# Positive part and square of each mixer step on one engine, in place, in a ring of six slots

## The reference

```python
inv_norm = rsqrt(maximum(sum(xf * xf, -1), EPS));  xn = xf * inv_norm
sim = einsum('bic,bjc->bij', xn, xn)
sim = power(relu(sim), 2.0)              # positive part, then square
y = einsum('bij,bjc->bic', sim, t)       # t = x W
x = x + y
```

## Time and profile before

| | us |
|---|---|
| median of 3 runs | 4165.13 |
| lowest and highest run | 4151.47 and 4180.86 |
| span of the profiled execution | 4159.1 |
| PE busy in it | 3515.1 (85%) |
| VectorE busy | 3096.5 (74%) |
| ScalarE busy | 2399.5 (58%) |
| GpSimd busy | 1974.2 (47%) |
| mean granted TensorE clock | 0.900 of full |

### The profile page before, as it was taken

How to read it: one execution, slowest core, us unless ns; L and a number is a source line. 1 busy time by engine, 2 the same in 40 slices (tenths; PEclk the granted TensorE clock), 3 DMA queues, 4 the chain that set the end, 5 groups by cost and what they waited for, 6 DMA issues and landing times.

```text
span 4159.1 us, 58338 instructions
## 1 busy us (share of the span) xinstructions
PE 3515.1 (85%) x21688; PEld 1896.4 (46%) x21688; DVE 3096.5 (74%) x4894; ACT 2399.5 (58%) x4152; POOL 1974.2 (47%) x1805
## 2 busy tenths in 40 slices
PE   5979997999899999999889999999899999946431
PEld 2434444454544445444544455444544455525321
DVE  6466477887788687877788678877688678865775
ACT  5755774577655775577556775577556775522210
POOL 0000074554456364555455463545455464657670
PEclk8989998999899999999899989999899989965555
DMA  4000122232222332231222332232222332234355
GB/s 112 1 8 1 40 82 67 74 99 56 71 83 80 78 89 64 75 98 58 79 77 74 79 96 56 77 92 64 74 79 70 81 86 65 83 103 117 101 123 113
DMA packets 374811, 314.92 MB, mean 76 GB/s; under 512 B 312672, under 2 KB 317024, under 8 KB 374528
## 3 DMA queue, kind: packets, MB, share of 16 engines
q0 software_dynamic: 85248, 231.33, 19.0%
q1 hardware_dynamic: 289280, 79.88, 8.9%
HBM read 279.30 MB, written 57.69 MB: 81 GB/s over the span
## 4 chain that ended last, share of the span: by engine, by line
PE 63%; DVE 16%; ACT 9%; DVEq 5%; issue 3%; DMA 2%; SPq 1%; POOL 1%; ACTq 0%
PE PS L1543 57%; DVE work L908 3%; PE PS L1747 3%; DVEq L492 3%; DVE G L496 2%; PE PS L1579 2%; DVE G L490 2%; DVE small L904 1%; ACT work L1363 1%; ACT work L1435 1%; ACT small L1408 1%; PE PS L1583 1%; ACT xn_hl L1281 1%; POOL G L452 1%; DMA out<-x 1%
## 5 line engine op out<-in xcount | busy, mean ns | idle before, releaser
L452 POOL DMA_INDIRECT G<-corner_table,index x1800 | 1973.6, 1096 | 2049.0 <-DVE values L498 737.5
L1435 ACT ACTIVATE work<-PS,descale 128x512 f32<-128x512 f32 (+2 forms) x896 | 566.7, 633 | 514.9 <-PE PS L1543 503.5
L1363 ACT ACTIVATE work<-PS 128x768 f32<-128x768 f32 (+2 forms) x800 | 651.1, 823 | 273.4 <-PE PS L1543 222.6
L908 DVE SCALAR_TENSOR_TENSOR work<-PS,descale,work 128x512 f32<-128x512 f32 (+2 forms) x896 | 605.7, 680 | 152.3 <-ACT work L1435 138.3
L818 DVE TENSOR_TENSOR work<-work 128x768 f32<-128x768 f32 (+2 forms) x496 | 480.1, 972 | 294.9 <-PE PS L1543 252.4
L1543 PE MATMUL PS<-work,xm 128*64 128x400 f32 (+3 forms) x3200 | 622.3, 502 | 0.0
L490 DVE TENSOR_TENSOR G<-G,corner_w 128x768 f32<-128x768 f32 x600 | 561.4, 951 | 43.5 <-DMA G<-corner_table,index 42.1
L1543 PE MATMUL PS<-xn_hl,xn_hh 128*128 128x384 f16 (+2 forms) x1600 | 539.2, 337 | 51.0 <-ACT work L1363 42.3
L1543 PE MATMUL PS<-xn_hl,xn_ll 128*128 128x384 f16 (+2 forms) x1600 | 534.0, 334 | 0.0
L1543 PE MATMUL PS<-work,w3s 128*64 128x384 f32 (+2 forms) x1792 | 439.8, 569 | 64.5 <-DVE small L904 64.5
L1543 PE MATMUL PS<-xn_hl,w1h 128*128 128x512 f16 (+2 forms) x896 | 319.5, 357 | 64.2 <-DVE work L908 55.6
(11 more groups left out here) (262 smaller groups left out, 4961.2 us busy)
## 6 DMA issues: line engine op xcount, KB each, us to landing
G<-corner_table,index POOLq DMA_INDIRECT x1800
corner_table<-rows_scratch SPq DMA_DIRECT2D x32, 784.0 KB
corner_table<-G SPq DMA_DIRECT2D x8, 841.0 KB, 8.5
xin<-x SPq DMA_DIRECT2D x8, 768.0 KB, 5.7
rows_scratch<-xln SPq DMA_DIRECT2D x8, 768.0 KB
x_scratch<-xB SPq DMA_DIRECT2D x8, 768.0 KB
yw_scratch<-yw SPq DMA_DIRECT2D x7, 784.0 KB, 6.4
x<-x_scratch SPq DMA_DIRECT2D x4, 784.0 KB, 6.0
```

What stands on the lines that cost most here:

```text
L452: GP.indirect_dma_start(G[0:rows, n % 2, tap * 4 * C:(tap + 1) * 4 * C], None, tables[b % 2], bass.IndirectOffsetOnAxis(ap=index[0:rows, c ...
L908: V.scalar_tensor_tensor(hid[:, e % 4, 0:w], S[2 + e % 2][:, 0:w], descale[:, MOE2:MOE2 + 1], silu[:, e % 2, 0:w], ALU.mult, ALU.mult).the ...
L1363: A.activation(relu[0:rows, u % 2, :, 0:n], PS[u % 2][0:rows, :, 0:n], ACT.Relu).then_inc(s["relu_done"], 1)
L1435: A.activation(silu[:, e % 2, 0:w], S[e % 2][:, 0:w], ACT.Silu, scale=descale[:, MOE1:MOE1 + 1]).then_inc(s["silu_done"], 1)
```

## The change

`ACT_STEPS` becomes (0, 2, 3, 4, 6, 7). An engine that has a step now takes its positive part from PSUM and squares it, in place, in one ring `sq` of `SLOTS` = 6 slots, indexed by the global step number. VectorE has steps 1 and 5 alone: positive part (L820 of the changed kernel), a drain, square (L822). ScalarE has the six others: positive part L1369, square L1375. `squares_taken` lets a slot be written once the `mix` of six steps earlier is done. TensorE waits for `relu_done` or the new `relu_dve`, by who has the step (`taken`). ScalarE's list changes in order too: in step u it takes the positive part of u (not u + 1), then squares u - 1, then does its other work of (j, u).

```diff
-ACT_STEPS = (0, 3, 6)
+ACT_STEPS = (0, 2, 3, 4, 6, 7)
...
-        relu = work[:, 0:4 * IWM].rearrange("p (q b n) -> p q b n", q=2, b=2)
-        sq = work[:, 4 * IWM:12 * IWM].rearrange("p (q b n) -> p q b n", q=4, b=2)
+        sq = work[:, 0:2 * SLOTS * IWM].rearrange("p (q b n) -> p q b n", q=SLOTS, b=2)
...
-            return 2 * half_no + n - 1
+            return 2 * half_no + n + 3 - SLOTS
...
                             if u in DVE_STEPS:
-                                dve.wait_ge(s["relu_done"], g + u + 1)
+                                dve.wait_ge(s["sim_done"], g + u + 1)
                                 free = squares_taken(hn, g + u)
                                 if free > 0:
                                     dve.wait_ge(s["mixed"], free)
...
+                                V.tensor_scalar(v, sim, 0.0, None, ALU.max).then_inc(s["relu_dve"], 1)
+                                dve.drain()
+                                V.tensor_tensor(v, v, v, ALU.mult).then_inc(s["sq_dve"], 1)
...
-            def relu_step(s_no, half, jh, u):
+            def relu_step(s_no, hn, half, jh, u):
                 rows, n = tile_rows(jh * JB + u // 2), IWS[half]
                 act.wait_ge(s["sim_done"], s_no + 1)
...
+            def square_step(s_no, hn, half, jh, u):
+                rows, n = tile_rows(jh * JB + u // 2), IWS[half]
+                act.wait_ge(s["relu_done"], square_act(hn, jh, u))
+                v = sq[0:rows, s_no % SLOTS, :, 0:n]
+                A.activation(v, v, ACT.Square).then_inc(s["sq_act"], 1)
...
                             if u in ACT_STEPS:
...
+                                relu_step(g + u, hn, half, jh, u)
+                            if u - 1 in ACT_STEPS:
+                                square_step(g + u - 1, hn, half, jh, u - 1)
+                            if u == 0 and jh and SPB - 1 in ACT_STEPS:
+                                square_step(g - 1, hn, half, jh - 1, SPB - 1)
...
+            def taken(hn, jh, u):
+
+                if u in ACT_STEPS:
+                    pe.wait_ge(s["relu_done"], square_act(hn, jh, u))
+                else:
+                    pe.wait_ge(s["relu_dve"], square_dve(hn, jh, u))
...
                                 if not last:
-                                    pe.wait_ge(s["relu_done"], g + u + 1)
+                                    taken(hn, jh, u)
                                     sims(half, jh * JB + (u + 2) // 2, u)
```

More of the change, by code:

```diff
@@ L64, in metaformer_kernel @@
     NW = 6
+    SLOTS = 6
     ACT_N = len(ACT_STEPS)
@@ L195, in metaformer_kernel @@
             f_centered f_squared f_var f_std f_scaled f_cast f_split f_tr f_cm
-            sim_done relu_done sq_act sq_dve mixed z_ready y_done
+            sim_done relu_done relu_dve sq_act sq_dve mixed z_ready y_done
             logits_done sm_shift sm_exp disp_split disp_tr disp_cm
@@ L817, in mixer @@
                                     dve.wait_ge(s["mixed"], free)
-                                V.tensor_tensor(sq[0:rows, u % 4, :, 0:n], relu[0:rows, u % 2, :, 0:n], relu[0:rows, u % 2, :, 0:n],
-                                                ALU.mult).then_inc(s["sq_dve"], 1)
+                                sim = PS[u % 2][0:rows, :, 0:n]
+                                v = sq[0:rows, (g + u) % SLOTS, :, 0:n]
+                                V.tensor_scalar(v, sim, 0.0, None, ALU.max).then_inc(s["relu_dve"], 1)
+                                dve.drain()
+                                V.tensor_tensor(v, v, v, ALU.mult).then_inc(s["sq_dve"], 1)
                             if k >= 1:
@@ L1358, in ffn_prepare @@
                         ffn_evac(f, c)
-            def relu_step(s_no, half, jh, u):
+            def relu_step(s_no, hn, half, jh, u):
                 rows, n = tile_rows(jh * JB + u // 2), IWS[half]
                 act.wait_ge(s["sim_done"], s_no + 1)
-                A.activation(relu[0:rows, u % 2, :, 0:n], PS[u % 2][0:rows, :, 0:n], ACT.Relu).then_inc(s["relu_done"], 1)
-            def squared(hn, jh, u):
-                if u in DVE_STEPS:
-                    act.wait_ge(s["sq_dve"], square_dve(hn, jh, u))
-                else:
-                    act.wait_ge(s["sq_act"], square_act(hn, jh, u))
+                free = squares_taken(hn, s_no)
+                if free > 0:
+                    act.wait_ge(s["mixed"], free)
+                A.activation(sq[0:rows, s_no % SLOTS, :, 0:n], PS[u % 2][0:rows, :, 0:n], ACT.Relu).then_inc(s["relu_done"], 1)
+            def square_step(s_no, hn, half, jh, u):
[3 more added lines that the diff above has]
+                A.activation(v, v, ACT.Square).then_inc(s["sq_act"], 1)
             def mixer(k):
@@ L1374, in mixer @@
                     g0, hn, n = k * SPI + half * SPH, k * 2 + half, IWS[half]
-                    relu_step(g0, half, 0, 0)
                     for jh in range(BPH):
@@ L1663, in sims, with mix @@
                 ins.then_inc(s["sim_done"], 1)
-            def mix(half, hn, jh, u):
+            def taken(hn, jh, u):
[3 more added lines that the diff above has]
+                    pe.wait_ge(s["relu_dve"], square_dve(hn, jh, u))
+            def mix(g, half, hn, jh, u):
                 j, n = jh * JB + u // 2, IWS[half]
@@ L1673, in mix @@
                 for b in range(2):
-                    ins = mm((Y0, Y1)[u % 2][b * C:(b + 1) * C, 0:n], xm[0:rows, j, :], sq[0:rows, u % 4, b, 0:n], False, False)
+                    ins = mm((Y0, Y1)[u % 2][b * C:(b + 1) * C, 0:n], xm[0:rows, j, :], sq[0:rows, (g + u) % SLOTS, b, 0:n], False, False)
                 ins.then_inc(s["mixed"], 1)
@@ L1704, in mixer @@
                             if v:
-                                mix(half, hn, jh, v - 2)
-                                mix(half, hn, jh, v - 1)
+                                mix(g, half, hn, jh, v - 2)
+                                mix(g, half, hn, jh, v - 1)
                             elif jh:
-                                mix(half, hn, jh - 1, SPB - 2)
-                                mix(half, hn, jh - 1, SPB - 1)
-                    mix(half, hn, FULL, 0)
-                    mix(half, hn, FULL, 1)
+                                mix(g - SPB, half, hn, jh - 1, SPB - 2)
+                                mix(g - SPB, half, hn, jh - 1, SPB - 1)
+                    mix(g0 + FULL * SPB, half, hn, FULL, 0)
+                    mix(g0 + FULL * SPB, half, hn, FULL, 1)
                     if not half:
-                        pe.wait_ge(s["relu_done"], g0 + SPH)
+                        taken(hn, FULL, 0)
+                        taken(hn, FULL, 1)
                         sims(1, 0, 0)
```

12 lines of the change are left out of this document (removed).

## The result

| | before | after |
|---|---|---|
| median | 4167.03 us (4 runs) | 4260.36 us (4 runs, 4258.26 to 4263.72) |
| ratio | | 1.0221, interval 1.0199 to 1.0243 |
| span of the profiled execution | 4159.1 us | 4258.9 us |

What follows compares the result with a forecast made beforehand. PE (TensorE) was taken to bound the mixers. Late reads of 10.1 us per image, less 1.0, plus 0.3, gave 56 us for images 2 to 7; with image 1's 3.9, 60 on 4165.1: 4225 us, range 4145 to 4280.

Steps and rivals of the forecast that it cites:

- What bounds, and the mechanism: In the mixers: PE sets the time, and VectorE's step 1 read, taking 0.97 us, comes late behind `sample_add`.
- The places: Late PSUM reads in blocks 1, 4, 5 and 7 to 12 make PE wait, 10.1 us per image in sum.
- Blocks 7 and 8: VectorE has no idle time there, so its own chain delays step 1 of block 8: 1.35 us for both blocks.
- Block 5: Behind the shorter second `offsets_tm`, the read of step 0 comes one read later: 0.75 us.
- steps 5: VectorE's reads of step 5 have slack, with two squares fewer and one read more ahead: no term added.
- What comes back: PE's waits for positive parts in the mixers shrink as ScalarE stops waiting for VectorE's squares: 1.0 us back per image.
- my sum: Per image 10.1 us lost, 1.0 back, 0.3 for ScalarE's queue; 56 us for images 2 to 7, 60 in total.
- Block 4: VectorE's read for step 1 stands behind `positions_floor`, so PE goes on later: 1.75 us.
- Bounds: Outside the sum: two more places per image at 1.2 GHz, 20 us more, 4245; ScalarE's added work everywhere, 4298.
- The gain: Rival: rings decouple and VectorE reaches step 1 early, so the 42.3 us of PE's waits vanish: 4113 us, chance 0.1.
- ScalarE as the bound: Rival: ScalarE's later list and full pairs in blocks 1, 11 and 12 hold PE: 4245 to 4298 us, chance 0.15.
- my own case: Whole kernel slower through late reads in the mixers: 4206 to 4245 us, chance 0.45.

Runs made afterwards that it cites:

- the kernel with two reads ahead: Kernel before with only the six-slot ring, plus ScalarE reading step 1 of the next block too ahead of `offsets_tm` at (3, 7) and (4, 7): 4148.82 us, ratio 0.9945.
- the dose: Changed kernel plus one unused `memset` of 896 elements on VectorE at u = 0 of blocks 9 to 12, images 2 to 7: 4293.82 us, ratio 1.0303.

## Why the prediction was right in its direction and short in its size

**What bounds, and the mechanism: right.** PE's products in the mixers set the time, and what came was what the working followed: VectorE's read of step 1, in an in-order list behind `sample_add` and the work of u = 0. L820 took 0.955 us (768 elements) and 0.988 us (800) by shape, 0.971 in the mean, where I took 0.97. The trace agrees with what the Trainium skill, "VectorE: DVE Perf Modes", "Why PSUM operands drop a tier", states: an fp32 operation with an operand in PSUM runs at the single rate.

```profile
L820 DVE TENSOR_SCALAR work<-PS 128x800 f32<-128x800 f32 x96 | 94.8, 988 | 53.0 <-PE PS L1539 52.8
...
L820 DVE TENSOR_SCALAR work<-PS 128x768 f32<-128x768 f32 x96 | 91.7, 955 | 143.7 <-PE PS L1539 143.5 <-issue 0.2
```

PE's waits for L820 were 54.0 us (I gave 50 to 70), and blocks 2 and 3 had none.

**The places: nearly all smaller than said.** Blocks 1, 9, 10, 11 and 12 were put at 1.0, 1.7, 1.5, 1.05 and 1.0 us, and took 0.77, 1.52, 1.26, 0.79 and 0.80: 5.1 instead of 6.25 us. A share of it is the 0.47 us from the product of `dcn_cm` to L503. At block 11 the product starts at 2020.02, so it was 0.36 there. Blocks 7 and 8 were put at 1.35 us more than before; in image 4 the waits for L820 of 0.98, 0.45 and 0.96 us stand where 1.66 us for ScalarE had stood, 0.7 more. Block 5 was put at 0.75 and took 0.70. I had given steps 5 slack; that did not hold everywhere: step 5 of block 7 made PE wait 0.45 us in image 4, and 2.20 and 2.27 us in images 5 and 7.

**What comes back: wrong.** I let ScalarE's waits shrink by 1.0 us an image, and said that they would be less than now apart from block 4. They grew from 42.3 to 45.2 us. A ScalarE list that is one step later stood in front of PE near the head of the half (1.39 us, where it had been 0.31; not in my sum), at block 4 and, with some 0.3 us each, at several pairs between. **Block 4** was in the sum for 1.75 us by VectorE's read behind `positions_floor`. PE waited 2.95 for ScalarE's read behind `offsets_tm` and then 0.27 for VectorE's, against 2.19: 1.0 more, and of the other engine. I had written that what ScalarE reads "is ready earlier". It was the later one for PE, since PE asks for step 0 first. With ScalarE's read put ahead, VectorE's place came out as in my sum: 4.24 - 2.19 = 2.05 us, where I had 1.75.

These misses nearly cancel. In image 4 the terms of the sum came to 7.6 us instead of 10.1, and the rest to 1.8 us more instead of 0.7 less: 9.4 us of idle time, just as the sum had it. Over all mixers it was 58.5 us, where the sum had 60. That agreement is luck: the places on VectorE were too large and ScalarE's too small.

**The step that failed: the clock.** The sum took PE's busy time as given. The prediction put the clock under "Bounds", at most two more places an image at 1.7 us each, "20 us more", and took nothing of it. Measured: PE's busy time in the mixers rose by 39.5 us, and the clock's record has 73.7 - 40.4 = 33.3 us of it as time at the lower level. The rest came at full clock, and what made it is open. With the busy time, 60 becomes 93 to 100, which is the result. My reason was that the new waits of 1.0 to 1.75 us "are shorter" than the one of 2.19 us after which the clock fell. For blocks 9 to 12 that reason held, as their clock of 1.00 shows. The trace has the clock at half rate in two other kinds of place in image 4. Behind block 4, there for 3.4 us as before, though in images 1, 2, 5 and 7 for 6.8; then over the first 7 us of half 1, where waits of about 1 us follow on the idle time at the change of halves:

```profile
1921.00:1923.00 2.00, 1.26 (x4) 0.43 (x4) 1.75 (x5) 2.00 (x3) 0.00 (x0) 0.64 0.00 0
...
1962.00:1964.00 2.00, 1.06 (x6) 0.29 (x3) 1.84 (x4) 0.90 (x2) 1.39 (x3) 0.63 0.28 92
1964.00:1966.00 2.00, 1.96 (x6) 0.89 (x7) 1.73 (x3) 0.75 (x2) 1.69 (x2) 0.50 0.38 119
1966.00:1968.00 2.00, 2.00 (x7) 0.71 (x5) 1.73 (x3) 2.00 (x4) 0.09 (x1) 0.50 0.24 78
```

At that head of half 1 the clock was at 1.2 GHz for 6.8 us; before it was 3.4. In 1964 to 1968 PE was busy nearly all the time and still at half rate. I read this as short waits prolonging a slow stretch that was already there; that is not shown, and the kernel with two reads ahead, which is slow there without such waits, speaks against it as the whole cause. The Trainium skill, "TensorE: Matmul & The Clock Gate", "A second HAM failure mode: psum-queue depth-cycling", says that in one kernel short idle times between groups of matmuls, frequent enough, made the clock go back and forth between its levels. The runs agree in part: in blocks 9 to 12 the clock fell behind nine of the twelve dosed waits of 2.14 to 2.75 us and behind none of the 36 of 0.79 to 1.67 us of the two kernels. Had I read it beside rows 10, the clock would have had a place in the sum and not only in the bounds.

**The rivals.** The gain was tied to L503 starting early, and it did not start before PE's product, as said. It had a true part, though: the ring by itself frees ScalarE (0.25% faster). ScalarE as the bound, by its added work, did not happen: the same work with both reads early costs nothing. Its waits came from its order. I had put both in one case and priced it by load.

**The size.** 4260 lies above my own case (4206 to 4245), in what I had given to ScalarE as the bound (4245 to 4298), and within the range; it got there by the clock and not by ScalarE's load. The halves of image 4 took 106.6 and 100.9 us, for 104 and 100.

**What stays open.** The waits of images 3 and 4 are nearly the same after the change (20.1 and 19.6 us of waits over 0.1 us), and the mixers took 210.4 and 207.5 us at a clock of 0.95 and 0.96. What decides whether a given wait lowers the clock was not settled. Open too is why the change of halves is slow for longer after the change, and why block 0 lost 7.5 us to the clock in this profile and 1.4 in that of the dose, whose work there is the same. Shown is that adding idle time alone, with the same products, makes them slower where it makes waits of over 2 us.

## What to carry to other kernels

When an operation that reads PSUM moves to another engine, or to a later place in its own engine's list, price it by what stands ahead of it in that list and by when the writer wants the buffer back; that the new engine has time to spare says nothing. Mend both readers of a handshake at once: mending one gave back half of the loss or less here, because the writer then waits for the other. And where TensorE is the bound, look at the length of each wait and not only at their sum: waits of 0.8 to 1.5 us cost little more than their own length here, and 19 us that made some of them longer than 2.1 us cost 33.

## What the runs showed of the hardware that I had not expected

PE's idle time had a second price, and it depended on where it fell. Added idle time of 58.5 us in the mixers came with 39.5 us more busy time for the same products, and 19.4 us with 10.7 (the dose). Of the dose's waits in blocks 9 to 12, nine of twelve of 2.14 to 2.75 us had 3.4 us at 1.2 GHz behind them, and none of twelve of 1.67 us; the change's own 24 of 0.79 to 1.52 us there had none. These are counts of two profiles and no limit. Less idle time than before gave nothing back: with 53.1 us instead of 72.4 PE's busy time stayed at 1442 us, and the record had even 7 us more at the lower level.
